# Gated mixture kernel on Trainium2: first expert product transposed and woven with the preceding pair's second product

## What is computed

```python
def _L0_xattn_ref(hidden_states, token_ids, Wg, Wu, Wd):   # Wg = Wu = Wd = ctx
    expert_ids = jnp.minimum(tid // tokens_per_expert, E - 1)
    for e in range(E):
        g = jax.nn.silu(jnp.einsum('bsd,fd->bsf', hidden_states, Wg[e]))
        u = jnp.einsum('bsd,fd->bsf', hidden_states, Wu[e])
        y = jnp.einsum('bsf,df->bsd', g * u, Wd[e])
        out = jnp.where((expert_ids == e)[..., None], y, out)
    return out

x = x + jnp.tanh(g_xattn[0]) * _L0_xattn_ref(_layernorm(x, axis=-1), tok, ctx, ctx, ctx)
x = x + jnp.tanh(g_ffn[0]) * _L0_ffn_ref(_layernorm(x, axis=-1), Wr, br, Wd, bd, Wu, bu)
```

## Time and profile before

| | |
|---|---|
| median of 3 runs | 202.97 us (202.61 to 202.98) |
| span of the profiled execution, first to last instruction | 201.4 us |
| mean granted TensorE clock | 0.974 |
| PE busy | 175.0 us (87%) |
| DVE busy | 155.7 us (77%) |
| ACT busy | 111.9 us (56%) |
| POOL busy | 99.7 us (50%) |

### The profile page before, as it was taken

How to read it: one execution, slowest core, us unless ns; L and a number is a source line. 1 busy time by engine, 2 the same in 40 slices (tenths; PEclk the granted TensorE clock), 3 DMA queues, 4 the chain that set the end, 5 groups by cost and what they waited for, 6 DMA issues and landing times.

```text
span 201.4 us, 4382 instructions
## 1 busy us (share of the span) xinstructions
PE 175.0 (87%) x1074; PEld 104.0 (52%) x1075; DVE 155.7 (77%) x523; ACT 111.9 (56%) x224; POOL 99.7 (50%) x246
## 2 busy tenths in 40 slices
PE   1576896999997989999999999999999999976560
PEld 1564463655553656656656556655665655534310
DVE  4859696697768799889888998797877878678640
ACT  2596599884287166473665726547265561545200
POOL 4478846427246366375553735516244162445641
PEclk9999999999999999999999999999999999999955
DMA  5947572101210201203101011011010100101121
GB/s 135 370 163 231 205 216 69 52 5 20 86 55 0 52 0 52 59 0 104 55 0 54 0 52 52 2 52 52 0 54 0 52 20 33 52 0 55 52 104 52
DMA packets 6784, 13.43 MB, mean 67 GB/s; under 512 B 2392, under 2 KB 2520, under 8 KB 6768
## 3 DMA queue, kind: packets, MB, share of 16 engines
q0 software_dynamic: 2560, 8.39, 12.6%
q1 hardware_dynamic: 4208, 4.86, 7.3%
HBM read 9.06 MB, written 4.19 MB: 66 GB/s over the span
## 4 chain that ended last, share of the span: by engine, by line
PE 44%; issue 18%; POOL 10%; DVE 9%; DMA 7%; ACT 4%; DVEq 3%; SPq 2%; POOLq 1%; ACTq 0%
PE ps_y L603 6%; PE ps_y L605 6%; PE ps_y L604 6%; PE ps_a L603 4%; PE ps_a L605 4%; PE ps_a L604 4%; DMA xs<-in_x_dram,rows_of 4%; ACT h L796 3%; POOL rs L457 3%; PE ps_h2T L685 2%; PE ps_pT L624 2%; DMA bu_nat<-in_L_ffn_bu_dram 2%; POOL hot_slot L432 2%; PE ps_hT L677 2%; POOL xs L439 2%
## 5 line engine op out<-in xcount | busy, mean ns | idle before, releaser
L456 POOL TENSOR_SCALAR ve<-mv 128x1 f32<-128x1 f32 x32 | 7.7, 239 | 62.6 <-DVE mv L1099 51.8
L796 ACT ACTIVATE h<-xs,mrs,rs 128x512 f32<-128x512 f32 (+1 forms) x16 | 21.1, 1317 | 22.4 <-POOL mrs L458 22.4
L783 ACT ACTIVATE pT_hi<-ps_pT 128x512 f16<-128x512 f32 x19 | 11.3, 595 | 36.0 <-PE ps_pT L624 36.0
L603 PE MATMUL ps_y<-w_hi,pT_hi 128*128 x76 | 28.8, 379 | 2.3 <-DVE w_lo L952 1.5
L603 PE MATMUL ps_a<-w_hi,hT_hi 128*128 x76 | 29.1, 382 | 0.7 <-DVE hT_lo L1074 0.6
L604 PE MATMUL ps_a<-w_lo,hT_hi 128*128 x76 | 29.1, 382 | 0.0
L605 PE MATMUL ps_a<-w_hi,hT_lo 128*128 x76 | 29.0, 381 | 0.0
L604 PE MATMUL ps_y<-w_lo,pT_hi 128*128 x76 | 28.8, 379 | 0.0
L605 PE MATMUL ps_y<-w_hi,pT_lo 128*128 x76 | 28.8, 379 | 0.0
L1086 DVE SCALAR_TENSOR_TENSOR xs<-ps_y,y_t,xs 128x512 f32 x19 | 14.3, 750 | 10.2 <-PE ps_y L605 7.7
L529 POOL DMA_INDIRECT out_dram<-xs,rows_of x16 | 17.3, 1083 | 5.9 <-DVE xs L1117 3.5
(11 more groups left out here) (209 smaller groups left out, 424.0 us busy)
## 6 DMA issues: line engine op xcount, KB each, us to landing
w_nat<-in_ctx_dram SPq DMA_DIRECT2D x4, 1024.0 KB, 7.9
xs<-in_x_dram,rows_of POOLq DMA_INDIRECT x16, 3.6
wd_nat<-in_L_ffn_Wd_dram SPq DMA_DIRECT2D x1, 256.0 KB
wu_nat<-in_L_ffn_Wu_dram SPq DMA_DIRECT2D x1, 256.0 KB
out_dram<-xs,rows_of POOLq DMA_INDIRECT x16, 2.9
b_in<-in_L_ffn_bd_dram SPq DMA_DIRECT2D x1, 64.0 KB
bu_nat<-in_L_ffn_bu_dram SPq DMA_DIRECT2D x3, 16.0 KB
tok_i<-in_itok_BxS_dram SPq DMA_DIRECT2D x1, 8.0 KB, 1.8
```

The source lines that it names most:

```text
L603: mm(ps[:, :], lhs_hi[:, kc, :], hi, start=(kc == 0), stop=False)
L796: a(h2[:, :, :], x1[:, col(k), :].rearrange("p o (q c) -> p c (o q)", c=KC), ACT.Identity, bias=mrs[:, 1, col(k)], scale=rs[:, 1, col(k)]) ...
```

## The change

The first product is computed transposed: the expert's weights, in 128 x 128 blocks, are stationary and the `hT` blocks (128 columns) move, so that `ps_a` holds the product with features on partitions and `prod` comes out in the layout that the second product needs. The four transposes of `prod` and their bank `ps_pT` are gone for the pairs; `pT_hi` and `pT_lo` are made from `prod` itself. The first product is now 48 matmuls of 128 columns in four blocks of 12, and after each block comes a quarter (3 matmuls of 512 columns) of the second product of the pair before. On PE `y(i-1)` thereby moves from near the end of step i to its middle, and `low_rank_out` moves behind the transposes of `h(i+1)`. ACT makes `pT_hi(i)` behind `hT_hi(i+1)` in step i instead of at the start of step i+1. DVE does `product(i)`, `add_y(i-1)`, `hT_low(i+1)`, `pT_low(i)`, `h2T_low(i-5)`, the addition of tile i-7, `statistics2`, `hidden`. One weight block's bank moves from `ps_y` to `ps_pT`. Special orders for the last steps on DVE and PE are dropped.

```diff
+        prodT = prod[:, :].rearrange("p (c q) -> p c q", c=KC)
...
-                   [ps_o, ps_y, ps_h2T, ps_wT], [ps_h2T, ps_wT, ps_o, ps_hid]]
+                   [ps_o, ps_pT, ps_h2T, ps_wT], [ps_h2T, ps_wT, ps_o, ps_hid]]
...
+            def second_product_block(kc, e):
+
+                hi = w_hi[:, bass.ds(e, 1), kc, :].rearrange("p e n -> p (e n)")
+                lo = w_lo[:, bass.ds(e, 1), kc, :].rearrange("p e n -> p (e n)")
+                mm(ps_y[:, :], pT_hi[:, kc, :], hi, start=(kc == 0), stop=False)
+                mm(ps_y[:, :], pT_hi[:, kc, :], lo, start=False, stop=False)
+                return mm(ps_y[:, :], pT_lo[:, kc, :], hi, start=False, stop=(kc == KC - 1))
+
+            def first_product_block(m, e):
+
+                cols = slice(m * P, (m + 1) * P)
                 for kc in range(KC):
-                    hi = w_hi[:, bass.ds(e, 1), kc, :].rearrange("p e n -> p (e n)")
...
+                    hi = w_hi[:, bass.ds(e, 1), kc, cols].rearrange("p e n -> p (e n)")
+                    lo = w_lo[:, bass.ds(e, 1), kc, cols].rearrange("p e n -> p (e n)")
+                    mm(ps_a[:, cols], hi, hT_hi[:, kc, :], start=(kc == 0), stop=False)
+                    mm(ps_a[:, cols], hi, hT_lo[:, kc, :], start=False, stop=False)
+                    last = mm(ps_a[:, cols], lo, hT_hi[:, kc, :], start=False, stop=(kc == KC - 1))
                 return last
...
+            def products(i, has_a, has_y, e_now, e_last):
+
+                if has_a:
+                    if isinstance(i, int) and i < E:
+                        wait_low(pe, i)
+                    pe.wait_ge(hT_lo_done, i + 1)
+                for n in range(KC):
+                    if has_a:
+                        a_last = first_product_block(n, e_now)
+                        if n == KC - 1:
+                            a_last.then_inc(a_done, 1)
+                    if has_y:
+                        if n == 0:
+                            before_second(i - 1)
+                        y_last = second_product_block(n, e_last)
+                        if n == KC - 1:
+                            y_last.then_inc(y_done, 1)
...
-                if has_y and has_a:
-                    transpose_product(i - 1)
...
+                products(i, has_a, has_y, e_now, e_last)
                 if meanwhile:
                     meanwhile()
...
-                if has_y and has_a:
-                    second_product(i - 1, e_last)
...
+                if some(NP, 0, i0):
+                    k = i
+                    act.wait_ge(prod_done, k + 1)
+                    wait_last(act, y_done, k)
+                    a(pT_hi[:, :, :], prodT, ACT.Copy).then_inc(pT_hi_done, 1)
...
-                v.tensor_tensor(pT_lo[:, :, :], ps_pT[:, :, :], pT_hi[:, :, :],
+                v.tensor_tensor(pT_lo[:, :, :], prodT, pT_hi[:, :, :],
...
                 if some(NP, 0, i0):
                     product(i)
+                if some(NP, -1, i0):
+                    add_y(i - 1, *place(i - 1))
                 if some(NP, 1, i0):
                     hT_low(i + 1)
-                if some(T, -2 - LATE, i0) and not draining:
+                if some(NP, 0, i0):
+                    pT_low(i)
...
+                if some(T, -2 - LATE, i0):
                     h2T_low(i - 2 - LATE)
```

More of the change, by code:

```diff
@@ L616, in second_product @@
                 if isinstance(k, int) and k == 0:
[L617 to L625, removed]
+                    pe.wait_ge(*low_done(1, w_banks[1].index(ps_y)))
+            def products(i, has_a, has_y, e_now, e_last):
[14 more added lines that the diff above has]
+                            y_last.then_inc(y_done, 1)
             def hidden_product(k):
@@ L678, in step @@
                     last.then_inc(hT_done, 1)
-                if has_y and not has_a:
-                    second_product(i - 1, e_last)
+                if some(T, -4 - LATE, i0) and has_a:
+                    low_rank_out(i - 4 - LATE)
                 if some(T, -2 - LATE, i0):
@@ L776, in step @@
             def step(i, i0, meanwhile=None):
[L779 to L783, removed]
                 if meanwhile:
@@ L856, in _ @@
             ffn_high_parts()
-            pipeline(act, step, 5, (-1, 0, 1, 2), (2, -2 - LATE, -3 - LATE, -4 - LATE))
+            pipeline(act, step, 5, (0, 1, 2), (2, -2 - LATE, -3 - LATE, -4 - LATE))
         @block.vector
@@ L1126, in step @@
             def step(i, i0, meanwhile=None):
-                ending = some(NP, -1, i0) and not some(NP, 0, i0)
                 draining = not some(NP, -1, i0)
-                next_ends = some(NP, 0, i0) and not some(NP, 1, i0)
-                if ending:
-                    pT_low(i - 1)
-                    statistics2(i - 2 - LATE)
-                    hidden(i - 3 - LATE)
                 if some(T, -3 - LATE, i0):
@@ L1152, in step @@
                                     ALU.subtract).then_inc(wtT_lo_done, 1)
-                if some(NP, -1, i0) and not ending:
-                    pT_low(i - 1)
                 if meanwhile:
@@ L1158, in step @@
                     statistics1(i + 3)
-                if some(T, -2 - LATE, i0) and draining:
-                    h2T_low(i - 2 - LATE)
-                if ending:
-                    add_y(i - 1, *place(i - 1))
-                    statistics2(i - 1 - LATE)
                 if some(T, -3 - LATE, i0):
@@ L1185, in step @@
                     add_low_rank(i - 4 - LATE)
-                if not ending:
-                    if some(NP, -1, i0):
-                        add_y(i - 1, *place(i - 1))
-                    if some(T, -1 - LATE, i0) and not next_ends:
-                        statistics2(i - 1 - LATE)
-                if some(T, -2 - LATE, i0) and not next_ends:
+                if some(T, -1 - LATE, i0) and some(NP, 0, i0):
+                    statistics2(i - 1 - LATE)
+                if some(T, -2 - LATE, i0):
                     hidden(i - 2 - LATE)
```

22 lines of the change are left out of this document (4 added, 18 removed).

## The result

| | before | after |
|---|---|---|
| median | 202.79 us (202.55 to 202.98, 4 runs) | 267.85 us (266.37 to 268.78, 4 runs) |
| span of the profiled execution | 201.4 us | 266.5 us |
| mean granted TensorE clock | 0.974 | 0.864 |
| PE, DVE busy | 175.0 and 155.7 us | 190.9 and 155.4 us |

The ratio is 1.321 [1.315, 1.326]. The direction was forecast, the size was not: 235.5 us (226 to 245) was predicted.

A forecast was written before the change was run, and what follows sets the result against it. PE work laid end to end, 8.46 us a step, bounded the kernel before; afterwards a chain through DVE. Span 201.4 plus 24.4, 3.7, 4.2 and 0.3 gave 234.0, plus 1.5 for the median: 235.5 us (226 to 245).

The forecast's parts named there:

- the cover: PE's 4.67 us of other work between a and the next hidden product, hiding some 2.8 us; 2.7 us left after.
- The cycle of a loop step, 10.84: Chain from a through silu, product, add_y, hT_lo, pT_lo, h2T_lo and hidden product to the next a: 10.84 us.
- Matmul pitch 0.056: First product on PE: each 128-column matmul takes 0.056 us, so 48 take 2.68 in place of 2.59.
- The sequencer's pace: Upper end for the first product's price on PE: 0.236 us per group of three matmuls, 3.8 us for sixteen groups.
- The 0.3 us for a product with no hidden product ahead of it: Added for the first block on PE, where issue takes 0.95 us against 0.67 of array work.
- Outside the loops the wait is in the engine's queue, the loads run early, and 0.67 stands: On DVE outside the loops, add_y comes 0.67 us after the product; such a step takes 9.54 us.
- Each load taken at 0.31: In loop steps add_y's two table loads begin at the product's start; add_y comes 1.78 us after it, not 0.67.
- Rival 1: Table loads in DVE's sequencer stay hidden, read past the waiting product: 8 x 1.11 less, 226.6 us; chance 0.12.
- Rival 4: TensorE's clock drops to 1.2 GHz for part of the steps, some 5 us each: above 245 us; chance 0.04.
- Start, +4.2: Before a(3): a(2) 0.8 us later, weight block transposed later +3.0, add_y ahead of hT_lo 0.67; bounds +2 and +6.
- End, +0.3: From a(18) to the last instruction, before 32.8 us: 0.3 us longer, bounds -1.5 and +2.
- Rival 3: Faster: the chain stays under PE's work, each of 13 steps costs 8.06 us, total 201.6; chance 0.03.

The follow-up runs named there:

- Experiment 4: Kernel before, with h2T_low moved on DVE behind add_y and statistics2 so that PE must wait at the hidden product; 245.47 us, ratio 1.206.
- experiment 1: Kernel before with only the first product transposed (48 matmuls of 128 columns, no transposes of prod), no weave, engine orders as before; 207.54 us, ratio 1.019.
- experiment 8: Kernel after, with ten discarded matmuls of 512 columns as filler in PE's wait ahead of each hidden product; 252.59 us.
- experiment 10: Kernel after reordered: DVE does h2T_low before pT_low and add_y last, ACT h2T_hi before pT_hi, PE transposes h2 before low_rank_out; 241.04 us, ratio 1.185.
- experiment 9: Kernel after, with the table loads ahead of the product and six discarded 512-column matmuls in PE's wait; 236.00 us, ratio 1.162.
- experiment 2: Kernel after, with add_y's two table loads on DVE read ahead of the product instead of behind it; 240.63 and 246.52 us.
- experiment 5: experiment 2 with PE's hidden product moved from ahead of a into the weave, behind the second quarter of y; 254.31 us.
- experiment 11: experiment 10 with add_y's two table loads put apart, one behind h2T_lo and one behind pT_lo; 231.18 us, ratio 1.137.

## Why the prediction was right in its sign and wrong in its size

- **What bounded the kernel before, and that the cover is gone:** right; the trace of after shows PE waiting 2.8 us for `h2T_lo` in each step. Experiment 4 makes such a wait in the kernel before by another edit, and it costs 42 us.
- **The cycle of a loop step, 10.84:** right. 10.81, 10.77 and 10.87 in the steps at the full clock where the loads took no longer than in the earlier trace rows. The wait at the hidden product is 2.8 us on average, at the upper end of the predicted 1.3 to 2.8.
- **Matmul pitch 0.056:** right (4.57 for 4.56). The Trainium skill's 81 ns at 128 columns (TensorE: Matmul & The Clock Gate, Back-to-back issue gap) is not what a stream took here. The sequencer's pace, which the prediction named as the upper bound, shows in full only where no y stands between the blocks (experiment 1). The 0.3 us for a product with no hidden product ahead of it was low: 0.46 to 0.55 (experiment 8).
- **"Outside the loops the wait is in the engine's queue, the loads run early, and 0.67 stands":** wrong, 4.7 us from a(5) to a(18) and 1.8 in the two steps before. The place of the wait does not decide it: with the wait on the register instruction or on the product itself, the loads start when silu is done and the product starts. DVE's timeline of step 7, outside the loops, and the first load:

```profile
106.71 0.75 DVE L1074 SCALAR_TENSOR_TENSOR prod<-ps_a,prod_bits,silu 128x512 f32<-128x512 f32 x1 [2.95 <-ACT silu L806]
108.25 0.75 DVE L1092 SCALAR_TENSOR_TENSOR xs<-ps_y,y_t,xs 128x512 f32 x1 [0.80 <-issue]
```

```profile
L1085 DVEq TENSOR_LOAD <-pair_tile_i x1: 301/301/301, 106.7 to 106.7; - x1
```

What holds DVE's sequencer is a semaphore that is not yet met, not the number of instructions ahead. In the earlier trace rows the first load ran at 106.9, while `h2T_lo` (107.07) and the addition (107.67) ahead of it had not started; `h2T_hi`, for which `h2T_lo` waits, had ended at 106.63. In experiment 10 the loads stand behind `pT_lo`, and the first began at 121.5, when `pT_hi` had ended at 121.40, before `pT_lo` started at 121.63:

```profile
120.77 0.63 ACT L819 ACTIVATE pT_hi<-prod 128x512 f16<-128x512 f32 x1
```

```profile
L1083 DVEq TENSOR_LOAD <-pair_tile_i x1: 575/575/575, 121.5 to 121.5; - x1
```

This rule is read from these places; no run was made to test it.

- **Each load taken at 0.31:** low in the loops, 1.5 us. The second of a pair often took more (DVE's sequencer, step 9):

```profile
L1086 DVEq TENSOR_LOAD <-source_i x1: 594/594/594, 130.7 to 130.7; - x1
```

- **Rival 1 (the loads stay hidden), 0.12:** refuted; they were exposed in all steps.
- **Rival 4 (the clock falls), 0.04:** this is what happened, and the step that failed. The prediction took 65% busy at a clock of 1.00 in 180 to 190 us as evidence that a PE with gaps keeps its clock. That was one stretch of 10 us directly before the clock fell, while the kernel before had nowhere a long run of steps with a gap in each. Its trace could not show that such a run holds, so this rival should have had a chance of its own size, with "above 245" inside the range. The sum thus put the loss of clock at nothing. It is some 12 us in the 13 steps (12.6 by the trace, of which 0.5 is not the clock, and 12.1 in experiment 8), and 15.3 us of the whole in experiment 8. The Trainium skill (TensorE: Matmul & The Clock Gate, HAM oscillation) tells of a kernel whose clock falls anew at every tile because PE waits there each time. The trace here agrees in kind, but the clock fell in only some of the steps: seven of the 13 products were slow.
- **Start, +4.2:** +7.1 measured. Between a(2) and a(3) the clock is below 1 (slices of 7 and 8), where the estimate had 1.00: a(2) took 5.96 us for the 5.00 of a(1). How the rest of the 2.9 us divides between clock and order was not tried apart.
- **End, +0.3:** +5.7. a(18) itself took 6.22 us for 4.57 by the clock, and with filler alone (experiment 8) the end took 35.5 of the 38.5, so 3.0 are the clock. The other 2.7 above before's 32.8 were not taken apart; they stay with the loads early too (35.8 in experiment 9).
- **Rival 3 (faster):** no version with the weave came near it. The best of them is 231.2 us.

## What to carry to other kernels

Before an operation is woven into another, measure what the moved work was covering: here the second product hid silu and three DVE operations. The transposed product alone costs 4 us (experiment 1), and a wait at the hidden product alone costs 42 (experiment 4); the weave without the transposed product was not run, so that moving y is the cause of the rest is argued from these two and from the waits in the trace. An exposed wait in every step can have a second price in TensorE's clock, and filler in the gap shows that price at once. Register loads belong ahead of the instruction whose semaphore comes late, not directly behind it.

## What the runs showed of the hardware

- DVE's sequencer stood at an instruction until its semaphore was met, and otherwise ran ahead of the engine by two instructions (the first load at 106.9 with `h2T_lo` at 107.07 and the addition at 107.67 still to start). Two register loads from a table behind an instruction that waits put 1.54 to 2.15 us between its start and that of the next in place of 0.67, in a loop or not; ahead of the waiting instruction they cost nothing (experiment 2), ahead of one that does not wait DVE stood 0.8 to 1.5 us (experiment 5), and spread over two instructions of 0.6 us they left 0.3 to 0.4 each (experiment 11).
- The granted clock fell to 0.50, the 1.2 GHz level, again and again in kernels whose PE waited 2.4 to 3.4 us in each step of some 11, with matmuls of 128 and of 512 columns alike, and was 0.99 from 87 to 228 us once discarded matmuls filled the gap (experiments 4 and 8).
- Small matmuls with addresses in registers came 0.056 us apart for 5 to 14 groups of three behind a hidden product, and then three of them took 0.24 us, the pace at which the sequencer issues them; in the first pairs that was the pace throughout (experiment 1).
